# Two V products in one key tile: where a block of matmuls stands in TensorE's written-out order

## The reference

```
xn = layernorm(x)
q, k, v = rope(xn @ Wq), rope(xn @ Wk), xn @ Wv      # 16 heads of 64; k and v have each column twice
out = softmax(q @ k.T * 2) @ v                       # per head, no mask, 1024 keys
ffn = (silu(xn @ Wg.T) * (xn @ Wu.T)) @ Wd.T         # 384 hidden
result = x + out @ Wo + ffn
```

## Time and profile before

| | |
|---|---|
| median of 3 runs | 1128.86 us (1128.25 to 1129.79) |
| profiled execution, its own time | 1127.29 us |
| its span, first to last instruction | 1125.4 us |
| mean granted TensorE clock | 0.991 of full speed |
| busy: TensorE matmul / weight load | 97% / 59% |
| busy: VectorE / ScalarE / GpSimd | 81% / 64% / 76% |

### The profile page before, as it was taken

The page is one execution under the profiler, slowest core; times in us unless marked ns, Lnnn a source line. Parts: engine busy times, 40 slices in busy tenths (PEclk is TensorE's granted clock), DMA queues, the critical chain, the costliest instruction groups (busy, mean ns, idle before and its releaser), DMA issues.

```text
span 1125.4 us, 17086 instructions
## 1 busy us (share of the span) xinstructions
PE 1090.5 (97%) x6288; PEld 661.9 (59%) x6288; DVE 912.1 (81%) x1023; ACT 722.1 (64%) x1327; POOL 853.3 (76%) x268
## 2 busy tenths in 40 slices
PE   5899999999999999999999999999999999999987
PEld 4787455666656565656656565656666565654533
DVE  7686878888888888888888888888888888887755
ACT  3333666666666676667666676667666676666664
POOL 3321878888888888888888888888888888888770
PEclk9899999999999999999999999999999999999998
DMA  6662907144260817154260817153260817140000
GB/s 238 159 246 101 269 1 196 38 150 121 48 186 2 232 38 205 29 142 129 50 183 2 232 38 205 29 155 117 51 183 2 232 38 202 32 109 26 4 2 19
DMA packets 56338, 124.98 MB, mean 111 GB/s; under 512 B 8000, under 2 KB 19520, under 8 KB 54080
## 3 DMA queue, kind: packets, MB, share of 16 engines
q1 hardware_dynamic: 56256, 123.90, 37.8%
HBM read 53.08 MB, written 10.49 MB: 56 GB/s over the span
## 4 chain that ended last, share of the span: by engine, by line
PE 93%; DVE 4%; ACT 2%; DMA 1%; issue 1%; ACTq 0%; DVEq 0%
PE bank_s L553 24%; PE scores L392 22%; PE bank_o L407 21%; PE scores L374 8%; PE bank_m L382 3%; PE bank_m L417 3%; PE bank_m L420 2%; PE bank_m L443 2%; PE scores L493 2%; PE bank_s L510 1%; PE bank_m L427 1%; PE bank_m L434 1%; DVE row_max L950 1%; PE bank_o L510 1%; PE bank_m L510 1%
## 5 line engine op out<-in xcount | busy, mean ns | idle before, releaser
L871 ACT ACTIVATE prob<-bank_s 128x512 f32<-128x512 f32 x992 | 566.2, 599 | 274.0 <-PE bank_s L553 263.9
L950 DVE TENSOR_REDUCE row_max<-scores 128x1 f32<-128x1024 f32 x512 | 601.2, 1215 | 97.0 <-PE scores L392 92.9
L1181 POOL TENSOR_TENSOR prob_sum<-prob_sum,prob 128x2048 f32<-128x2048 f32 x93 | 427.1, 4592 | 13.4
L553 PE MATMUL bank_s<-qk_pack 98*128 98x512 f32 x992 | 393.4, 427 | 3.4 <-ACT prob L871 2.0
L392 PE MATMUL scores<-qk_pack 96*128 96x512 f32 x1024 | 323.4, 402 | 2.4 <-DVE rope L945 1.7
L553 PEld LDWEIGHTS bank_s<-qk_pack 98*128 98x128 f32 x992 | 178.2, 188 | 176.2 <-ACT prob L871 117.5
L407 PE MATMUL bank_o<-prob,v 128*32 128x512 f32 x2048 | 254.4, 603 | 0.0
L392 PEld LDWEIGHTS scores<-qk_pack 96*128 96x128 f32 x1024 | 184.6, 189 | 61.1 <-DVE row_max L950 28.8
L1181 POOL TENSOR_TENSOR prob_sum<-prob_sum,prob_pair 128x2048 f32<-128x2048 f32 x31 | 142.5, 4596 | 80.9 <-DVE prob_pair L1043 80.9
L1173 POOL TENSOR_TENSOR prob_sum<-prob 128x2048 f32<-128x2048 f32 x31 | 142.2, 4587 | 0.0
L1125 POOL TENSOR_TENSOR qk_stage<-rope,qk_stage 128x512 fp32r<-128x512 f32 x64 | 81.8, 1280 | 77.9 <-ACT qk_stage L757 77.8
(11 more groups left out here) (105 smaller groups left out, 754.3 us busy)
## 6 DMA issues: line engine op xcount, KB each, us to landing
qk_pack<-qk_stage SPq DMA_DIRECT2D x384, 128.0 KB, 4.5
table<-tables SPq DMA_DIRECT2D x16, 2048.0 KB, 9.7
w_stage<-w_scratch SPq DMA_DIRECT2D x14, 640.0 KB, 4.7
v<-v_stage SPq DMA_DIRECT2D x32, 256.0 KB, 7.4
xT_scratch<-xT_hl SPq DMA_DIRECT2D x4, 1024.0 KB, 9.2
x_stage<-xT_scratch SPq DMA_DIRECT2D x4, 1024.0 KB, 6.6
w_scratch<-w_split SPq DMA_DIRECT2D x1, 2560.0 KB, 15.1
x_all<-x SPq DMA_DIRECT2D x4, 512.0 KB, 11.7
```

The lines of the kernel that those rows point to most:

```text
L553: mm(bank_s[:, h % 2, :], qk_pack[j][0:SCORE_K, 1, kt // QT, h, (kt % QT) * 128:(kt % QT + 1) * 128], qk_pack[j][0:SCORE_K, 0, t, h, :], s ...
L871: A(prob[:, kt % RING, h, :], bank_s[:, h % 2, :], ACT.Exp).then_inc(prob_ready, 1)
L950: V.tensor_reduce(row_max[:, m:m + 1], scores[:, at:at + 2, :].rearrange("p c k -> p (c k)"), axis=AX.X, op=ALU.max).then_inc(max_read, 1)
L1181: TT(prob_sum[:, t], prob_sum[:, t], part, ALU.add).then_inc(sum_done, 1)
```

## The change

In `slot`, the V product of key tile 2 no longer stands behind the second score of key tile 4, but ahead of the V product of key tile 3, behind the third score of key tile 5. The order of everything else is as it was, on all engines.

```diff
@@ -631,7 +631,6 @@
                         maximum(11)
                     elif kt == 4:
                         score(kt, 1)
-                        pv(u, 2, j)
                         score(kt, 2)
                         maximum(12)
                         score(kt, 3)
@@ -642,6 +641,7 @@
                         score(kt, 1)
                         maximum(14)
                         score(kt, 2)
+                        pv(u, 2, j)
                         pv(u, 3, j)
                         score(kt, 3)
                         maximum(15)
```

## The result

The changed kernel takes 1141.78 us (median of 4 runs, 1139.88 to 1144.02); the kernel before took 1129.32 beside it (4 runs, 1128.25 to 1135.23). The ratio is 1.0103, with a 95% interval of 1.0078 to 1.0129. The profiled execution took 1139.88 with a span of 1138.0, which is 12.6 us more than the span of before.

What follows compares the result with a forecast made beforehand. TensorE was taken as the bound, with no idle time in a slot. Per slot -0.46 + 0.06 + 0.86 = +0.46 us, times 31 is 14.3, on the median 1128.86 giving 1143.1 us; range 1138 to 1147.5.

Steps and rivals of the forecast that it cites:

- Term 1: Key tile 5: one more V product in the existing block there adds 0.86 us a slot.
- Term 2: Key tile 4, place emptied: score (4,2) waits for exp (4,0), so maximum 12 starts only 0.46 us earlier.
- Term 3: Ahead of score (5,0): maximum 13 waits for VectorE's row maximum of tile 11, +0.06 us a slot.
- 31 slots: Units 0 to 30 run the changed branch; each loses 0.46 us, carried whole into the next, 14.3 us in all.
- The lower bound: Maximum 13 waits for nothing, the matmul behind score (4,2) comes sooner: 0.33 us a slot, 1139.0 us.
- Behind the block: After key tile 5's V products, all TensorE waits for follows its own earlier work, so 0.46 us carries over.
- The merge pays: Rival: one block entry and exit less a slot saves 0.34 us, score (4,2) doesn't wait; 1118.3 us, chance 0.04.
- Given back: Rival: something downstream takes up the slot's loss; wholly, 1129 us, chance 0.03; in part, near 1136, chance 0.06.
- The ring: Rival: exp (6,0) waits for V product 2 to read its probability buffer; 1158 us; this or further waits, chance 0.05.

Runs made afterwards that it cites:

- the third buffer: Against the changed kernel, score (4,2) is written to the free `bank_m`, so it waits for no exp; 1141.20 us, ratio 1.0124 to the kernel before.
- the kernel that won 0.07: Against the kernel before, score (4,1) is written to `bank_m`, so it does not wait for exp (3,3); 1131.15 us, ratio 1.0017.

## Why the prediction was right, point by point

**The sum.** 1143.1 was forecast, 1141.78 measured. The ratio times the median that the forecast started from, 1.0103 x 1128.86, is 1140.5, with 1137.7 to 1143.4 for its interval. In the traces, one execution of each kernel, the loss is 12.6 us where 14.3 was forecast.

**Term 1, +0.86.** The pair takes 1.85 us where one took 0.99. Right.

**Term 2, -0.46.** Score (4,2)'s load is 0.05 behind exp (4,0), maximum 12 at 608.37 - 606.87 = 1.50 behind score (4,0) as forecast. Right to the hundredth, and shown by itself where V product 2 stood behind score (4,2). But the term gave the exp a weight that it doesn't have alone: by the forecast's own sum, the exp without term 3 puts score (5,0) at 2.67 behind score (4,0), and the third buffer took its wait away without moving score (5,0) from 2.72. With the exp's wait gone, reduction 11 cost the same.

**Term 3, +0.06, was about 0.02 too large.** Maximum 13's load does wait for the reduction, but score (5,0) is at 609.58 - 606.87 = 2.71, not 2.73; score (5,3) at 6.27, not 6.29. With that a slot loses 0.44 us rather than 0.46, 0.6 us over 31 slots. The wait named in this term is, by the third buffer, the one that decides.

**The lower bound.** It took 0.30 us from score (4,2) to the matmul behind it, where the prediction's own rows give 0.34; measured are 608.37 - 608.03 = 0.34. With that the bound is 0.29 us a slot instead of 0.33, 1137.9 instead of 1139.0.

**31 slots.** 27 do as forecast: slots 1 to 27 lose 0.44 each, 11.8 us. Those at the two ends don't all: slot 0 is only 0.13 us longer and slot 28 only 0.12, though key tiles 4 and 5 lose 0.38 and 0.43 in them. The traces show where it goes. At the end of slot 0 stands the first maximum of the unit after the next, and its weight load waits:

```profile
140.68 0.30 PEld L392 LDWEIGHTS scores<-qk_pack 96*128 96x128 f32 x2 [2.09 <-DVE rope L945]
```
```profile
140.59 0.30 PEld L392 LDWEIGHTS scores<-qk_pack 96*128 96x128 f32 x2 [0.50 <-issue]
```

The first is before, the second after. The rotation named there had ended at 139.72; line 572 also waits for the transfers of the packed queries and keys, and the last of these lands at 140.62 and 140.53, 0.06 us ahead of the load in both. The idle time ahead of the load was 2.09 us before and is 0.50 now. It takes up the loss, and also most of the 1.35 us that key tiles 0 to 3 of this slot take longer in the changed kernel, which runs at half the clock there (111.6 to 118.2). In slot 28, which has no projections, it is the transpose of the maxima in key tile 6 whose load stands at the same distance behind the slot's start in both kernels (25.77 and 25.75 us); it waits for VectorE's conversion of the maxima, of which more below.

The kernel before also had half the clock (0.50 from 1082.2 to 1085.4) in the block of three V products of slot 30, 4.28 us for what takes 2.71 elsewhere, and the changed kernel had not. That costs nothing in the end: the first score of the last unit starts 1.2 us sooner behind slot 30's start in the changed kernel, but the 13th 0.41 us later (42.40 against 41.99), since the load of the denominators between them, which waits for ScalarE, takes the difference up: it waits 2.45 us before and 3.95 after. The forecast of 14.3 less the 0.6 of term 3 is 13.7, 1.1 over the 12.6 measured. Of this, slots 0 and 28 account for 0.6, a start of attention 0.23 us sooner for another 0.2, and slot 30 and the last unit, 0.30 us longer together, for 0.1.

**Behind the block.** The prediction said that all that TensorE waits for there comes out of its own work, and moves with it. The loss is indeed carried whole from slot to slot from 1 to 27, but the reason was put too broadly: VectorE's chain behind the last maximum does not move with TensorE, see below. In those slots it had no effect because a later TensorE only gives that chain room. In slot 28 it took part of the loss back.

**The rivals.** "The merge pays" had the merge's price right (0.30 and 0.33 measured in two kernels against 0.34) and was out because the exp isn't hidden, nor is reduction 11. Even the 1118.3 it offered would not have been reached: the third-buffer kernel took its exp wait away, and nothing came of it. "Given back" happened in two slots of 31, 0.3 us in each, and not in the others: these are longer by all that key tiles 4 and 5 lost. "The ring" did not happen: exp (6,0) follows its score at the same distance as before, 0.51 us.

## What to carry to other kernels

Matmuls between two producers of the same buffer are cover: before one is moved to save a fixed cost, work out when the consumer's release comes without it, by the end of that consumer's instruction and the measured distance to the next load. Then do the same for the next two waits in order, since they may come at almost the same time, as three did here, and taking away the first then wins nothing. A cost that is real and separately measured (here 0.3 us for each block) is worth only what is left when the cover it buys is paid for.

## What the runs showed of the hardware that I had not expected

VectorE's conversion of the row maxima (line 956) has 16 elements a partition. It took 1.13 us before, 0.68 in the changed kernel, and 1.22 in the kernel that won 0.07. The timelines of VectorE and GpSimd, before:

```profile
608.91 1.13 DVE L956 CAST max_hl<-row_max 128x16 fp32r<-128x16 f32 x1
```
```profile
605.42 4.59 POOL L1181 TENSOR_TENSOR prob_sum<-prob_sum,prob 128x2048 f32<-128x2048 f32 x1
```

and in the changed kernel:

```profile
615.42 0.68 DVE L956 CAST max_hl<-row_max 128x16 fp32r<-128x16 f32 x1
```
```profile
611.47 4.58 POOL L1181 TENSOR_TENSOR prob_sum<-prob_sum,prob 128x2048 f32<-128x2048 f32 x1
```

The conversion ends at 610.04 and 616.10, GpSimd's addition at 610.01 and 616.05. In slots 2 to 28 of each of the ten traces it ends 29 to 42 ns behind GpSimd's addition, whenever it starts, and is shown as 0.31 to 1.26 us long. Where no addition is under way when it starts, as in slots 29 and 30, it takes 0.17 to 0.18 us. Slot 29 of the kernel before, VectorE and then GpSimd, whose addition ends at 1049.76:

```profile
1050.43 0.18 DVE L956 CAST max_hl<-row_max 128x16 fp32r<-128x16 f32 x1
```
```profile
1045.17 4.59 POOL L1181 TENSOR_TENSOR prob_sum<-prob_sum,prob 128x2048 f32<-128x2048 f32 x1
```

So the conversion waits for that instruction, though no semaphore says so, and 0.95 of its 1.13 us in the kernel before are this wait. The Trainium skill ("SBUF — State Buffer", "SBUF: two separate sides") says that the port pair which VectorE in some forms and GpSimd share is an exclusive lock, held for a whole instruction. This case's traces agree as far as the waiting goes, with these 0.03 to 0.04 us; that it is the port is the page's reading, no run here shows it.

It has a consequence. The sums on VectorE behind the conversion and the rotation come without a gap, and in the kernel before maximum 1's load of the next slot starts 0.05 us behind the rotation's end (615.61 + 0.69 = 616.30), at the end of every slot from 3 to 26:

```profile
615.61 0.69 DVE L945 TENSOR_TENSOR rope<-scores,rope 128x512 f32<-128x512 f32 x1
```
```profile
616.35 0.33 PEld L392 LDWEIGHTS scores<-qk_pack 96*128 96x128 f32 x2
```

That 0.05 us is the distance at which a load follows what it waits for. In the changed kernel the same load comes 0.37 to 0.44 us behind the rotation: TensorE is the later one there by what it lost, and the chain has room.

The chain hangs on GpSimd's addition, which a gain of TensorE in key tile 4 does not bring forward within the slot. In the kernel with score (4,1) in a third buffer the conversion starts as far behind score (5,3) as before but takes 1.22 us instead of 1.13, and maximum 1's load is again 0.05 behind the rotation's end in every slot. In slots 9 to 12 the rotation ends 0.06 to 0.13 us later behind the slot's start than before, and score (1,0) is 0.04 to 0.12 later, which takes back the 0.07. This is read from the traces; GpSimd's addition was not moved in a run of its own. So TensorE, busy without a gap in the kernel before, had a second limit beside it at no distance, and a small gain in key tile 4 could not have shown.
